# Output projection in twelve pieces in slots 9 to 14 of a layer's attention pipeline; second norm, routing and slot table one period later

## The chip, the cores and the metric

The kernel runs on one core of a Trainium2 chip, and its time is the device time of one execution in microseconds (us). The profile calls the engines PE (TensorE, matrix products; PEld is its weight loads), DVE (VectorE), ACT (ScalarE), POOL (GpSimd) and SP (SyncE, which only issues transfers here; SPq is its queue). Each engine runs its own instructions in program order, and engines wait for each other on semaphores.

## The reference

The reference makes 256 token rows per sequence with a state-space kernel, appends 128 text rows, and runs one transformer layer over 8 sequences of 384 rows of 512 values. The state-space part is a phase of its own and is not touched.

```python
h = jnp.concatenate([state_space(x), txt], axis=1)                  # (8, 384, 512)
h = h + attention(layernorm(h), Wq, Wk, Wv, Wo)                     # 16 heads of 32, 4 key/value heads
h = h + ffn(layernorm(h), gate_w, w_gate, w_up, w_down, ...)        # 64 experts, top 6, 64 slots each
...
scores = jnp.einsum('bhqd,bhkd->bhqk', q, k) * scaling
out = jnp.einsum('bhqk,bhkd->bhqd', softmax(scores), v)
attn = jnp.einsum('bsh,oh->bso', out, Wo)                           # the output projection
...
topk_w, topk_i = jax.lax.top_k(softmax(x @ gate_w.T), 6)            # routing
pos = position of each (token, expert) pair among the pairs of its expert
valid = pos < 64                                                    # a pair has a slot, or is dropped
```

## The kernel before

The program has three phases: the state-space phase, the attention phase, and the experts' phase, which starts when the attention phase has ended. The change is in `attention_phase` alone.

**A software pipeline over sequences.** The attention phase takes one sequence of 384 rows (NT = 3 tiles of 128) at a time. The outer loop runs over b, and each pass, called a period here, works on up to four sequences at once: b itself (`main`: scores, exponentials, values), the next, a = b + 1 (`nxt`: its projections, its rotary turn, its row maxima), the one before, c = b - 1 (`prev`: output projection, residual, second norm), and d = b - 2 (`prev2`: router logits, top 6, positions, slot table). Passes in which a role has no sequence leave it out.

**Slots.** Each period has NH = 16 slots, n = 0 to 15, one for each head. Each engine has the same loop over b and n, written by hand, with `if` lines that say what it does in which slot. That alone sets the order on an engine. On TensorE a slot starts with `scores(b, n)` (L634), three matmuls over 97 rows into PSUM banks 0 to 2. ScalarE then takes the exponentials (L808), and `values` (L650) multiplies them with the values and with ones four heads at a time, in three of every four slots: slots 3, 7, 11 and 15 have none.

**Row maxima.** The softmax needs each row's maximum ahead of the scores. In slots 8 to 15 TensorE computes the scores of the next sequence a first time, in bf16 (`raw`, L664), 48 units in all, six a slot, into two PSUM banks in turn. VectorE reduces each (`row_maximum`, L951). Unit u can't start before the maximum of unit u - 2 has been taken. The maxima are transposed in slot 12 and in slot 0 of the next period (`turn_maxes`, L670) and join the score matmuls as their 97th row.

**Around the change.** `project_out(c, s)` multiplies tile s of the attention output, split into a high and a low part (`out_hi` on ScalarE, `out_lo` on GpSimd, both after `divide` on VectorE), with the weights: 12 matmuls of 512 columns through `product`. It is done in slots 6, 7 and 8 (`OUT_SLOT`), and VectorE adds the residual one slot later. `statistics2` (L975) in slot 9, a power on GpSimd (L1108) and three activations (L870) give the normed rows x2; `turn_x2` (L724) transposes them in slots 12 to 15, each step waiting for ScalarE's copy (L876) of the one before, as all share PSUM bank 7. In the next period follow the router `logits` (L731) in slot 0, `routing` on VectorE in slots 1, 2, 4, 5 and 9, whose middle part (L996 to L1002) builds a mask of the chosen experts, and `places` (L739) on TensorE in slot 4. GpSimd works the positions out (L1081 to L1087) in slot 6. VectorE turns them into slot numbers in slot 9, and GpSimd scatters them into the slot table with 18 indirect DMAs (L1114), three in each of slots 10 to 15.

**Heads.** `rope` on VectorE and `rope_sum` on GpSimd (L1072) turn the queries and keys of the next sequence, one tile at a time. In slot 7 `turn_heads` (L706) transposes them in five steps; ScalarE copies each twice and VectorE takes the low part (`q_lo`, L940), and a step waits for the one two before it. The first raw scores wait for all of that.

## Time and profile before

| | us |
|---|---|
| Median of 3 runs | 1705.49 (1704.61 to 1706.07) |
| The profiled execution's own time | 1706.95 |
| Its span in the profile | 1705.3 |
| TensorE busy | 1368.9 |
| VectorE busy | 759.1 |
| ScalarE busy | 404.9 |
| GpSimd busy | 424.6 |

### The profile page before, as it was taken

The numbers are of one execution on the slowest core, as the hardware profiler recorded it, in microseconds if no ns is written. First come the engines' busy times: TensorE is split into PE (matmuls) and PEld (weight loads), VectorE is DVE, ScalarE is ACT, GpSimd is POOL, SyncE is SP. The second block draws the span as 40 slices with busy tenths as digits, with TensorE's granted clock in tenths as the row PEclk, the third lists the DMA queues.
The fourth block names the chain that finished last, engine by engine and source line by source line (L and its number), as shares of the span: only waits on it lengthen the run. The fifth ranks groups of instructions, "written<-read, shape, count | busy, mean of one in ns | idle before, by whom it ended". The sixth has DMA issues, their size and how long they took to land. (4 is left out here: it accounts for less than half of the span.)

```text
span 1705.3 us, 23870 instructions
## 1 busy us (share of the span) xinstructions
PE 1368.9 (80%) x9120; PEld 843.2 (49%) x9120; DVE 759.1 (45%) x1633; ACT 404.9 (24%) x676; POOL 424.6 (25%) x455
## 2 busy tenths in 40 slices
PE   3094788879788788887978840499999999999994
PEld 2094452434426254352533430366666666666673
DVE  7982545455555656456455331332232222232231
ACT  2021123333333233333333410211111111111110
POOL 3000110100242223324233446122222222222221
...
DMA packets 129837, 239.54 MB, mean 140 GB/s; under 512 B 58056, under 2 KB 64088, under 8 KB 129752
## 3 DMA queue, kind: packets, MB, share of 16 engines
...
## 5 line engine op out<-in xcount | busy, mean ns | idle before, releaser
L951 DVE TENSOR_REDUCE at_maxes<-at_ps 128x1 f32<-128x384 f32 x384 | 196.4, 553 | 131.3 <-PE at_ps L664 122.6
L808 ACT ACTIVATE bulk<-at_ps 128x1152 f32<-128x1152 f32 x128 | 144.9, 1132 | 367.4 <-PE at_ps L634 367.1
L1313 PE MATMUL mo_ps<-mo_x2s,mo_sgu 128*117 128x384 f32 (+1 forms) x1152 | 221.2, 344 | 0.0
L1313 PEld LDWEIGHTS mo_ps<-mo_x2s,mo_sgu 128*117 128x117 f32 (+1 forms) x1152 | 198.7, 181 | 13.4 <-issue 13.1
L1534 POOL DMA_INDIRECT out_rows<-mo_y,mo_scatter_ix x64 | 91.4, 1428 | 399.6 <-DMA out_rows<-mo_y,mo_scatter_ix 226.1
L664 PE MATMUL at_ps<-at_qb 32*128 32x384 bf16 x384 | 125.7, 442 | 78.6 <-DVE at_maxes L951 59.5
L1114 POOL DMA_INDIRECT slot_table<-at_toki,at_si x144 | 141.2, 981 | 51.0 <-issue 48.3
L664 PEld LDWEIGHTS at_ps<-at_qb 32*128 32x128 bf16 x384 | 28.6, 96 | 211.0 <-DVE at_maxes L951 173.5
L624 PE MATMUL at_ps<-WxT,at_xT 128*128 128x512 f32 (+1 forms) x576 | 114.0, 351 | 17.4 <-ACT at_v L853 15.6
L634 PE MATMUL at_ps<-at_QT 97*128 97x384 f32 x384 | 115.5, 416 | 6.9 <-ACT bulk L808 6.9
L1076 POOL TENSOR_TENSOR at_oTs<-at_oT,at_oTs 128x384 fp32r<-128x384 f32 x32 | 32.1, 1002 | 352.0 <-ACT at_oTs L820 352.0
L624 PEld LDWEIGHTS at_ps<-WxT,at_xT 128*128 128x128 f32 x576 | 90.0, 192 | 48.7 <-issue 34.5
L1327 PE MATMUL mo_ps<-mo_sd,mo_hs 117*128 117x512 f32 (+1 forms) x432 | 105.5, 397 | 3.6 <-DVE mo_so L1476 3.6
L650 PE MATMUL at_ps<-bulk,at_v 128*32 128x384 f32 x768 | 103.1, 629 | 3.4 <-DVE at_oT L964 2.7
L371 PE MATMUL ss_psK<-ss_Q,bulk 64*64 64x64 f32 x2048 | 62.7, 222 | 49.4 <-DVE bulk L320 48.4
L650 PE MATMUL at_ps<-bulk,at_ones 128*32 128x384 f32 x768 | 96.3, 598 | 0.0
L1327 PEld LDWEIGHTS mo_ps<-mo_sd,mo_hs 117*128 117x128 f32 (+1 forms) x432 | 79.4, 188 | 26.2 <-DVE mo_so L1476 5.6
L1498 DVE SCALAR_TENSOR_TENSOR mo_hm<-mo_sil,mo_wcol,mo_ps 128x352 f32<-128x352 f32 x32 | 18.6, 581 | 163.4 <-ACT mo_sil L1426 163.4
L634 PEld LDWEIGHTS at_ps<-at_QT 97*128 97x128 f32 x384 | 75.2, 224 | 30.3 <-issue 16.7
L624 PE MATMUL at_ps<-WoT,at_oTs 128*128 128x512 f32 x288 | 85.4, 453 | 5.4 <-DVEq L1015 3.4
L1355 PE MATMUL mo_ps<-mo_wgu,mo_xgT 128*64 128x352 f32 x512 | 82.0, 474 | 9.4 <-DMA mo_wd<-in_L_ffn_w_down 9.4
L371 PEld LDWEIGHTS ss_psK<-ss_Q,bulk 64*64 64x64 f32 x2048 | 62.2, 139 | 49.9 <-issue 49.9
...
## 6 DMA issues: line engine op xcount, KB each, us to landing
...
```

The source lines that it names most:

```text
L371: m = T.matmul(psK[half, n % 2, i * STEP:(i + 1) * STEP], Pm[half, k % 2, t, h, :], basis, start=(t == 0), stop=(t == 3))
L624: m = T.matmul(out, xs[:, xa, k, x_cols], ws[:, wa, k, w_cols], start=(n == 0), stop=(n == 3 * KC - 1))
L634: m = T.matmul(ps[:, kt, 0:SEQ], QT[:, NH + h // REP, kt * P:(kt + 1) * P], QT[:, h, :], start=True, stop=True)
L650: m = T.matmul(ps[HD * j:HD * (j + 1), 3 + sums, 0:SEQ], w, PT[:, (REP * G + j) % RING, kt, :], start=(kt == 0), stop=(kt == NT - 1))
L664: T.matmul(ps[:, 5 + u % 2, 0:SEQ], qb[rows, r, s * P:(s + 1) * P], qb[rows, REP, :], start=True, stop=True).then_inc(raw_scores, 1)
L808: A.activation(PT[:, N % RING, :, :], ps[:, 0:NT, 0:SEQ], ACT.Exp, scale=float(HD) ** -0.5)\
L951: V.tensor_reduce(maxes[:, s, h:h + 1], ps[:, 5 + u % 2, 0:SEQ], AX.X, ALU.max, negate=True)\
L1114: G.indirect_dma_start(slot_table, bass.IndirectOffsetOnAxis(ap=si[:, m:m + 1], axis=0), toki[:, m // TOPK:m // TOPK + 1], None, bounds_ch ...
L1313: m = M.matmul(ps[0:SW[c], 5 + g, 0:SEQ], sgu[:, wa, g, k, SO[c]:SO[c] + SW[c]], x2s[:, xa, k, :], start=(k3 == 0), stop=(k3 == 3 * KC - 1))
L1327: m = M.matmul(ps[:, 7, :], hs[0:SW[c], xa, c, s * P:(s + 1) * P], sd[0:SW[c], wa, c, :], start=(k3 == 0), stop=(k3 == 3 * SC - 1))
L1355: m = M.matmul(ps[CAP * e:CAP * (e + 1), 1 + g, 0:I], xgT[:, k, CAP * e:CAP * (e + 1)], wgu[j][:, e, g, k, :], start=(k == 0), stop=(k == ...
L1534: G.indirect_dma_start(acc, bass.IndirectOffsetOnAxis(ap=scatter_ix[:, qix, e:e + 1], axis=0), y[:, jy, e, :], None, compute_op=ALU.add).t ...
```

## The change

The output projection of a tile is cut into four pieces of three matmuls. The twelve pieces of the three tiles go into slots 9 to 14, two a slot: one behind the second pair of raw scores, one behind the third. The outputs of the first two groups of heads are kept in a ring of four and split in slot 15, since the projection now reads the split buffer until slot 14. Residuals move to slots 11, 13 and 15. The second norm moves from slot 9 to slots 0 and 1 of the next period, the transposes of x2 to slots 3 and 4, the logits to slot 5, the routing to slots 6, 7, 9 and 10, the places to slot 8 (TensorE) and slot 10 (GpSimd). The slot numbers and the scatters move one period further, into slots 1 to 6 of the period of e = b - 3, and the loop gets one pass more. SyncE stores the turned rows before the scores' rows and moves the store of h behind the maxima's row.

```diff
-        OUT_SLOT = {6: 0, 7: 1, 8: 2}
+        OUT_FROM = 9
+        OUT_SLOT = {OUT_FROM + 1: 0, OUT_FROM + 3: 1, OUT_FROM + 5: 2}
+        TURN_SLOT = {3: (0, 1), 4: (2, 3)}
+        DIVIDED = {0: (-2,), 4: (-1,), NH - 1: (0, 1)}
...
-        ITERATIONS = range(-1, B + 2)
+            return tuple(0 <= b - k < B for k in range(-1, 4))
+
+        ITERATIONS = range(-1, B + 3)
...
+                    sp.wait_ge(x2T_ready, KC * (d + 1))
+                    sp.dma_start(x2T_dram[d], x2T[:]).then_inc(x2T_stored, 16)
...
-            def project_out(c, s):
-                if s == 0:
+            def project_out(c, i):
+
+                s, piece = i // 4, i % 4
+                if i == 0:
                     pe.wait_ge(ohi_ready, NKV * (c + 1))
                     pe.wait_ge(olo_ready, NKV * (c + 1))
                     wait(pe, pos_read, c)
-                wait(pe, h2_ready, NT * c + s)
-                product(ps[:, 7, :], oTs, slice(s * P, (s + 1) * P), WoT, slice(0, D)).then_inc(proj_done, 1)
+                if piece == 0:
+                    wait(pe, h2_ready, NT * c + s)
+                m = product(ps[:, 7, :], oTs, slice(s * P, (s + 1) * P), WoT, slice(0, D),
+                            range(3 * KC // 4 * piece, 3 * KC // 4 * (piece + 1)))
+                if piece == 3:
+                    m.then_inc(proj_done, 1)
...
+                    pieces = range(2 * (n - OUT_FROM), 2 * (n - OUT_FROM + 1)) if prev and OUT_FROM <= n < OUT_FROM + 6 else ()
                     if main:
                         scores(b, n)
+                    if prev2 and n in TURN_SLOT:
+                        turn_x2(d, TURN_SLOT[n][0])
...
+                    if prev2 and n == 8:
+                        places(d)
+                    for i in pieces[0:1]:
+                        project_out(c, i)
...
-                    if prev2 and n == 0:
+                    if prev2 and n == 5:
...
-                    if prev2 and n == 4:
-                        places(d)
-                    if prev and n in OUT_SLOT:
-                        project_out(c, OUT_SLOT[n])
...
-                    if prev and n >= NH - KC:
-                        turn_x2(c, n - (NH - KC))
+                    if prev2 and n in TURN_SLOT:
+                        turn_x2(d, TURN_SLOT[n][1])
                     for u in units[4:]:
                         raw(a, u)
+                    for i in pieces[1:2]:
+                        project_out(c, i)
...
+            def x2_copied(d, k):
+                act.wait_ge(x2_turned, KC * d + k + 1)
+                wait(act, x2T_stored, 16 * d)
+                A.activation(x2T[:, k, :], ps[:, 7, 0:SEQ], ACT.Copy).then_inc(x2T_ready, 1)
+
             def out_hi(G):
                 act.wait_ge(o_ready, G + 1)
                 wait(act, proj_done, NT * (G // NKV))
-                A.activation(oTs[:, 0, G % NKV, :], oT[:, G % 2, :], ACT.Copy).then_inc(ohi_ready, 1)
+                A.activation(oTs[:, 0, G % NKV, :], oT[:, G % NKV, :], ACT.Copy).then_inc(ohi_ready, 1)
...
-                    if n in (0, 4, 9, 13):
-                        G = NKV * b + {0: -2, 4: -1, 9: 0, 13: 1}[n]
-                        if 0 <= G < NKV * B:
-                            out_hi(G)
+                    if prev2 and n in TURN_SLOT:
+                        x2_copied(d, TURN_SLOT[n][1])
+                    for k in DIVIDED.get(n, ()):
+                        if 0 <= NKV * b + k < NKV * B:
+                            out_hi(NKV * b + k)
...
-                if n == 1:
+                if n == 6:
...
-                if n == 2:
+                if n == 7:
...
-                if n == 4:
+                if n == 10:
...
-                if n == 5:
+                if n == 9:
...
+            def slots(e):
+                dve.wait_ge(slot_rows_ready, e + 1)
+                link(V.tensor_reduce(sf[:], hv[:], AX.X, ALU.add), route_step)
+                wait(dve, scattered, 16 * NT * TOPK * e)
...
+                    if prev and n - 1 in OUT_SLOT:
+                        residual(c, OUT_SLOT[n - 1])
                     if n % REP == REP - 1:
                         divide(NKV * b + n // REP - 1)
-                    if prev and n - 1 in OUT_SLOT:
-                        residual(c, OUT_SLOT[n - 1])
                     if nxt and n == 0:
                         for k in range(KC):
                             x_lo(a, k)
+                    if prev2 and n == 0:
+                        statistics2(d)
+                    if prev3 and n == 1:
+                        slots(e)
...
-                    if prev2 and n == 6:
+                    if prev2 and n == 10:
                         places(d)
-                    if prev and n == 9:
-                        pool.wait_ge(var2_ready, c + 1)
+                    if prev2 and n == 0:
...
-                    if prev2 and n >= 10:
-                        pool.wait_ge(slots_ready, d + 1)
-                        for m in range(3 * (n - 10), 3 * (n - 9)):
+                    if prev3 and 1 <= n <= 6:
+                        pool.wait_ge(slots_ready, e + 1)
+                        for m in range(3 * (n - 1), 3 * n):
```

The line numbers of the changed kernel differ: L625 is its `product`, L730 `turn_x2`, L737 `logits`, L745 `places`, L954 `q_lo`, L965 `row_maximum`, L985 the residual, L1011 to L1017 the masks, L1090 `rope_sum`, L1094 `out_lo`, L1131 the scatters.

How TensorE's order changes is seen in slot 9 of a full period, with the last rows of slot 8 ahead of it. L634 are scores, L664 raw scores, L650 values, L624 and L625 the output projection. Before:

```order
L624 MATMUL at_ps<-WoT,at_oTs 128x512 x12
L664 MATMUL at_ps<-at_qb 128x384 x2
L634 MATMUL at_ps<-at_QT 128x384 x3
L664 MATMUL at_ps<-at_qb 128x384 x2
L650 MATMUL at_ps<-bulk,at_v 32x384 x4
L664 MATMUL at_ps<-at_qb 128x384 x2
L650 MATMUL at_ps<-bulk,at_ones 32x384 x4
L664 MATMUL at_ps<-at_qb 128x384 x2
L634 MATMUL at_ps<-at_QT 128x384 x3
```

After, the same slot, from its scores (slot 8 has no projection):

```order
L634 MATMUL at_ps<-at_QT 128x384 x3
L664 MATMUL at_ps<-at_qb 128x384 x2
L650 MATMUL at_ps<-bulk,at_v 32x384 x4
L664 MATMUL at_ps<-at_qb 128x384 x2
L625 MATMUL at_ps<-WoT,at_oTs 128x512 x3
L650 MATMUL at_ps<-bulk,at_ones 32x384 x4
L664 MATMUL at_ps<-at_qb 128x384 x2
L625 MATMUL at_ps<-WoT,at_oTs 128x512 x3
L634 MATMUL at_ps<-at_QT 128x384 x3
```

The block of twelve projection matmuls of slot 8 is gone, and slot 9 has two pieces of three, the first behind the second pair of raw scores and the second behind the third pair.

GpSimd's order from the scatters of one full period to its positions. Before (L1114 scatters, L1076 `out_lo`, L1072 rotary sums, L1081 to L1087 positions):

```order
L1076 TENSOR_TENSOR at_oTs<-at_oT,at_oTs 128x384
L1114 DMA slot_table<-at_toki,at_si 4096x1 x9
L1076 TENSOR_TENSOR at_oTs<-at_oT,at_oTs 128x384
L1072 TENSOR_TENSOR at_r<-at_r 128x640
L1076 TENSOR_TENSOR at_oTs<-at_oT,at_oTs 128x384
L1072 TENSOR_TENSOR at_r<-at_r 128x640 x2
L1081 TENSOR_TENSOR at_pos<-at_pos,at_slot 128x192
L1083 TENSOR_TENSOR at_pos<-at_pos,at_over 128x192
L1087 TENSOR_TENSOR at_hv<-at_hot,at_pos 128x384 x3
```

After (L1131 scatters, L1090 rotary sums, L1094 `out_lo`, L1125 and L1127 the second norm):

```order
L1094 TENSOR_TENSOR at_oTs<-at_oT,at_oTs 128x384 x3
L1125 TENSOR_TENSOR at_rstd<-at_ve,at_mhalf 128x3
L1127 TENSOR_TENSOR at_shift<-at_shift,at_rstd 128x3
L1131 DMA slot_table<-at_toki,at_si 4096x1 x6
L1090 TENSOR_TENSOR at_r<-at_r 128x640
L1131 DMA slot_table<-at_toki,at_si 4096x1 x3
L1094 TENSOR_TENSOR at_oTs<-at_oT,at_oTs 128x384
L1090 TENSOR_TENSOR at_r<-at_r 128x640
L1131 DMA slot_table<-at_toki,at_si 4096x1 x6
L1090 TENSOR_TENSOR at_r<-at_r 128x640
L1131 DMA slot_table<-at_toki,at_si 4096x1 x3
L1083 TENSOR_TENSOR at_rstd<-at_ve,at_mhalf 128x3
```

Fifteen of the eighteen scatters now stand ahead of the third rotary sum, where none stood, and the power of the second norm stands ahead of the first of them.

VectorE's order around slots 7 and 8 (L940 and L954 the low parts of the heads, L970 a residual, L951 and L965 row maxima). Before:

```order
L964 TENSOR_TENSOR at_oT<-at_ps,at_rsums 128x384
L970 TENSOR_TENSOR at_hr<-at_hr,at_ps 128x512
L940 TENSOR_TENSOR at_qlo<-at_ps,at_qhi 128x384 x5
L970 TENSOR_TENSOR at_hr<-at_hr,at_ps 128x512
L951 TENSOR_REDUCE at_maxes<-at_ps 128x1 x6
L970 TENSOR_TENSOR at_hr<-at_hr,at_ps 128x512
```

After (L1011 to L1017 the masks, L1027 to L1029 the positions):

```order
L979 TENSOR_TENSOR at_oT<-at_ps,at_sT 128x384
L954 TENSOR_TENSOR at_qlo<-at_ps,at_qhi 128x384 x5
L1011 TENSOR_TENSOR at_hot<-at_iota,at_mf 128x384 x3
L1016 TENSOR_REDUCE at_pos<-at_hot 128x192
L1017 CAST at_mask<-at_pos 128x192
L965 TENSOR_REDUCE at_maxes<-at_ps 128x1 x6
L1027 TENSOR_TENSOR at_pos<-at_ps,at_base 128x192
L1028 TENSOR_SCALAR at_over<-at_pos 128x192
L1029 TENSOR_TENSOR at_base<-at_base,at_ps 128x64
L965 TENSOR_REDUCE at_maxes<-at_ps 128x1 x6
```

The masks now stand between the low parts of the heads and the first row maxima, and the residuals left that place.

## Rows read from the trace of the kernel before

**Rows 1.** The page, part 1: busy time, share of the span, instructions, by engine.

```profile
PE 1368.9 (80%) x9120; PEld 843.2 (49%) x9120; DVE 759.1 (45%) x1633; ACT 404.9 (24%) x676; POOL 424.6 (25%) x455
```

**Rows 2.** Windows, b = 4: length, busy PE, PEld, DVE, ACT, POOL, clock, DMA.

```profile
608.00:643.78 35.78, 32.23 (x220) 21.71 (x219) 16.76 (x48) 12.33 (x24) 5.08 (x4) 0.90 0.53 133
643.78:659.66 15.88, 12.39 (x66) 9.03 (x65) 8.32 (x22) 7.16 (x14) 6.44 (x8) 0.89 0.00 1
659.66:665.46 5.80, 5.80 (x34) 2.93 (x34) 2.45 (x5) 0.33 (x1) 0.00 (x0) 1.00 0.71 148
665.46:674.46 9.00, 5.42 (x27) 1.41 (x25) 8.47 (x20) 1.54 (x2) 1.84 (x2) 0.74 0.57 158
674.46:679.89 5.43, 5.43 (x26) 1.53 (x25) 2.60 (x5) 3.24 (x4) 3.92 (x5) 0.50 0.01 0
679.89:685.54 5.65, 3.29 (x11) 1.10 (x9) 5.18 (x11) 1.13 (x1) 4.14 (x5) 0.80 0.02 0
685.54:694.36 8.82, 7.60 (x32) 2.35 (x31) 2.71 (x6) 1.94 (x3) 0.97 (x1) 0.50 0.02 4
694.36:710.39 16.03, 13.69 (x71) 4.97 (x69) 10.93 (x22) 6.56 (x10) 9.77 (x10) 0.71 0.01 0
```

**Rows 3.** Timeline of TensorE, period of b = 4: start, us, instructions, idle before.

```profile
645.83 3.08 PE L624 MATMUL at_ps<-WoT,at_oTs 128*128 128x512 f32 x12
...
666.90 0.85 PE L650 MATMUL at_ps<-bulk,at_v 128*32 128x384 f32 x8
...
674.46 1.33 PE L634 MATMUL at_ps<-at_QT 97*128 97x384 f32 x3
...
676.15 1.51 PE L650 MATMUL at_ps<-bulk,at_ones 128*32 128x384 f32 x8
...
683.50 0.96 PE L664 MATMUL at_ps<-at_qb 32*128 32x384 bf16 x2 [2.09 <-DVE at_maxes L951]
```

**Rows 4.** Timeline of TensorE: slots 6 and 8 of b = 0; starts of three periods.

```profile
252.16 0.69 PE L634 MATMUL at_ps<-at_QT 97*128 97x384 f32 x3
...
262.28 0.63 PE L664 MATMUL at_ps<-at_qb 32*128 32x384 bf16 x2 [0.64 <-ACT at_qhi L864]
...
307.24 1.33 PE L634 MATMUL at_ps<-at_QT 97*128 97x384 f32 x3
...
403.37 1.33 PE L634 MATMUL at_ps<-at_QT 97*128 97x384 f32 x3
...
915.17 1.33 PE L634 MATMUL at_ps<-at_QT 97*128 97x384 f32 x3
```

**Rows 5.** Timeline of GpSimd, period of b = 4.

```profile
644.68 1.56 POOL L1072 TENSOR_TENSOR at_r<-at_r 128x640 f32<-128x640 f32 x1 [4.65 <-DVE at_r L934]
...
676.60 0.98 POOL L1114 DMA_INDIRECT slot_table<-at_toki,at_si  x1 [0.30 <-issue]
```

**Rows 6.** Timeline of VectorE, b = 4: split of x, masks (first, last), statistics.

```profile
615.36 1.13 DVE L911 TENSOR_TENSOR at_xT<-at_ps,at_xT 128x384 fp32r<-128x384 f32 x2 [1.71 <-ACT at_xT L837]
...
625.36 1.49 DVE L996 TENSOR_TENSOR at_hot<-at_iota,at_mf 128x384 bf16<-128x384 f32 x3
...
629.19 0.26 DVE L1002 CAST at_mask<-at_pos 128x192 bf16<-128x192 f32 x1
...
671.03 1.87 DVE L975 BATCH_NORM_STATS2 at_bn<-at_hr 128x6 f32<-128x512 f32 x3
```

**Rows 7.** Timeline after the last scores: last scores, logits, projection, a copy, last scatter.

```profile
971.46 0.77 PE L634 MATMUL at_ps<-at_QT 97*128 97x384 f32 x3
...
974.94 2.89 PE L731 MATMUL at_ps<-gwT,at_x2T 128*128 128x64 f32 x24
...
988.19 5.46 PE L624 MATMUL at_ps<-WoT,at_oTs 128*128 128x512 f32 x12 [3.42 <-DVEq L1015]
...
1011.02 0.49 ACT L876 ACTIVATE at_x2T<-at_ps 128x384 f32<-128x384 f32 x1 [0.99 <-PE at_ps L724]
...
1061.81 0.97 POOL L1114 DMA_INDIRECT slot_table<-at_toki,at_si  x1 [0.30 <-issue]
```

103 lines of the change are left out of this document (44 added, 59 removed).

## The prediction

> **What bounds the kernel now.** The page's first part comes first [rows 1]. TensorE is busy for 1368.9 us of 1705.3 and VectorE for 759.1, so TensorE's stream is the one to follow. The attention phase runs a pipeline of eight sequences with one period for each. The next thing to find is what one period costs and where TensorE stands idle or slow in it.
>
> Periods are read from the first score matmul of each sequence. They start at 307.24 (b = 1), 403.37 (b = 2) and 915.17 (b = 7) [rows 4]. So b = 1 lasts 96.1 us, and b = 2 to 6 last 511.8 / 5 = 102.4 us each. That makes five equal periods, one that is different, one that the change leaves alone (b = 0), and a tail.
>
> The period of b = 4 is then cut at its slots, the stretches between one head's scores and the next [rows 2]. Slots 0 to 5 (35.8 us) are TensorE's own: 32.2 us busy at a mean clock of 0.90. Slots 6 and 7 (15.9 us) wait on the chain that turns the heads. Slots 8 to 15 (50.7 us) are mixed. In slot 9 VectorE is busy 8.5 of 9.0 us and TensorE 5.4; in slot 11 VectorE has 5.2 of 5.7. In slots 10 and 12 TensorE is busy but runs at 0.50 of its clock. A group of value matmuls takes 0.85 us at full clock and 1.51 at half, and half-clock scores take 1.33 against 0.69 [rows 3, 4]. So the second half loses time in two ways. TensorE waits for row maxima (2.09 us in slot 11 alone [rows 3]), and it works at 1.2 GHz after such waits.
>
> **Slots 0 to 5.** The logits (2.89 us [rows 7], 2.7 without the overlap) leave slot 0 and enter slot 5. The four groups of x2 transposes enter slots 3 and 4 at some 0.4 us each; half of them fall into the wait for the values' copy. The place matmuls (0.3) leave. The sum is +0.2, so 36.0 us. VectorE gets the second norm's statistics (1.9 us for their first step [rows 6], some 2.7 in all) and the slot columns (an estimate of 2.2) there, about 5 us, while it is busy for only 16.8 of 35.8 us [rows 2], so I cost them at nothing for VectorE itself.
>
> **GpSimd.** This queue isn't free. Its 18 scatters cost 0.98 + 0.30 = 1.28 us each [rows 5] and stood in slots 10 to 15, where nothing waited for them. Now fifteen are issued in program order before the third rotary sum, for which the head transposes of slot 7 wait. GpSimd can start them when VectorE has made the slots. VectorE's split of x ends at 616.5, 8.5 us into the period [rows 6]; with statistics and slots behind it that is 13.5 us. To this come 15 x 1.28 = 19.2 us, one output residue of 1.0, three sums of 1.56 [rows 5], and a wait of about 4.5 us, since the residue in slot 4 now stands behind the last x2 copy on ScalarE, which comes with the end of slot 4, and the scatters issued by then fill less than the time up to it. The total is 42.9 us. Slot 6 begins at 36.0, so the sum ends 6.9 us after it. Before, it ended at 646.24, which is 2.5 us after slot 6 began at 643.78 [rows 2, 5]. GpSimd is 4.4 us late there. The lower bound is no lateness (the wait vanishes and DMA issues run closer), the upper one 7 us.
>
> **Slots 6 and 7.** They took 15.9 us with two output projections of about 3 us in them, one of which stretched the chain of head transposes. In b = 0, where no projection stands there, slots 6 and 7 take 262.28 - 252.16 = 10.1 us [rows 4]. With GpSimd's lateness, part of which is covered by VectorE (which now has 1.7 us of routing before its work on the heads and is late by some 2.4 us itself), I take 14.0 us: 1.9 saved. The bounds are 10.1 + 2.4 = 12.5 and 17.
>
> **Slots 8 to 15.** A projection of 12 matmuls takes 3.08 us at full clock [rows 3] and 5.46 at mostly half [rows 7]. A piece of three is then 0.75 or 1.35 us. Of each slot, before [rows 2] and now:
> - Slot 8, 5.8 us: it loses a projection, but VectorE must now build the slot masks (625.36 to 629.45, 4.1 us [rows 6]) before its first row maximum. TensorE has two score matmuls' work and then waits about 3.4 us. Then six maxima of 0.55. I take 7.9 us.
> - Slot 9, 9.0 us: VectorE loses residual, statistics and slots, about 5 us. TensorE's own work with two pieces is 4.8 us at full clock, 8.0 at half. I take 5.9.
> - Slot 10, 5.4 us at half clock: with pieces 5.0 at full clock.
> - Slot 11, 5.65 us: the wait for VectorE's division stays (residual in front of it fits into the time it had free). The first piece stands behind the wait and not in it. I take 7.3, since the clock should fall there again; 5.9 if not.
> - Slot 12, 8.8 us: minus one group of transposes (0.8), plus two pieces. All slow it is 10.5, all fast 7.4. I take 8.4.
> - Slots 13 to 15, 16.0 us with three groups of transposes: slots 13 and 14 take 9.5 at full clock with four pieces, and 16 at half. Slot 15 keeps its division and six maxima, 5.6. I take 15.1.
>
> The sum is 49.6 us against 50.7 (7.9 + 5.9 + 5.0 + 7.3 + 8.4 + 15.1). The period comes to 36.0 + 14.0 + 49.6 = 99.6 us, 2.8 less, and five of them give 14. In b = 1 no routing, second norm or scatter is moved in yet, so slots 6 and 7 fall from 15.9 to 10.1, and slots 8 to 15 stay within 0.2 us: -5.6 us, 90.5 us.
>
> **The tail.** The program goes one iteration longer. Before, x2 of sequence 6 was transposed between the scores of b = 7, and its logits began at 974.94 [rows 7]. Now its last residual comes with slot 15 of b = 7, whose scores ran at 971.46 [rows 7]; the projection pieces go where the x2 chain held b = 7 up, so I put it at 970.5 on the old clock. Then division, statistics, GpSimd's power and three activations (8.5 us) follow, and four steps of transposing and copying, 0.99 + 0.49 = 1.5 us each, by the copy and its wait [rows 7]: the logits begin at 985. From logits to the last sequence's projection it was 988.19 - 974.94 = 13.3 us [rows 7]; one division no longer stands in that stretch, so 11 to 13. The projection then begins at 996 to 998, 8 us later. What follows it (statistics, 18 scatters, places, slots, 18 scatters up to 1061.81 [rows 7]) has the same order as before. A third block of 18 scatters (23 us, for sequence 5) now stands in the tail, but I expect it from 978 to 1002, while the chain above goes on without GpSimd. So +8 us, between +4 and +12.
>
> **Sum.** -14 - 5.6 + 8 = -11.6 us. The profiled execution took 1706.95 us around its span of 1705.3, 1.46 us over the median of 1705.49. 1706.95 - 11.6 = 1695.3, and against the median 1693.9. I round to 1694 us.
>
> **Rivals.**
> - The clock stays high (0.22). If the pieces let TensorE leave half clock early in slot 9 and keep it through slot 11's wait, slots 9 to 15 cost 3.5 us less. With no more than VectorE's lateness in slots 6 and 7 (1.5 less) that gives 94.6 us a period: five times 7.8, 8 in b = 1 (its 5.6 and some clock), less 8 in the tail, is 39 us gained, 1667. For it: the pieces fill slots where 5.4 us of 5.4 were busy with matmuls of a quarter of the array's columns or rows. The Trainium skill ("TensorE: Matmul & The Clock Gate", What's actually happening) says that the default state is throttled and activity releases the throttle. Slot 10, busy throughout at 0.50, shows that busy time alone did not do it here [rows 2].
> - The clock stays low (0.16), the slower side. Slot 8 now has a wait of over 3 us, before it TensorE has only transposes, and slots 11 and 15 keep theirs. If half clock holds in slots 9, 12 and 13 as in [rows 2] it did in 10 and 12, they cost 8.0 + 10.5 + 6.3, some 6 us more than in my sum. The period is 105.6 us: five times +3.2, no gain in b = 1 and +8 in the tail come to +24, 1729. It decides once it costs more than 2.5 us a period over my sum.
> - The third block of scatters is exposed (0.09). If its slots are ready 11 us later than I think, half of it adds to the end: +12 us, no change, 1706.
> - GpSimd isn't late and the clock is as forecast: 98.1 us a period, five times 1.5 less, 1686; this lies inside my case.
>
> **Chances and range.** My case, from 1682 to 1704, holds 0.50, and 0.03 is left for what I have not thought of. Over 0.2% (3.4 us), about what a measurement of this kernel can tell from none, counts as a difference. Faster: 0.22 and most of 0.50 make 0.69. Same: 0.12. Slower: 0.19. The range reaches almost to the high-clock case and about half of the way to the low-clock one: 1671 to 1714.
>
> **What would show it.** In the changed profile I expect periods of 99 to 100 us between first scores, and about 90 for b = 1. Slots 6 and 7 should be 14 us, with the head transposes released by GpSimd's rotary sum; if VectorE releases them, my GpSimd count is wrong. The wait for maxima in slot 8 should be over 3 us, released by VectorE behind the masks. Granted clock in slots 9 to 14 should be above 0.75. The last projection should start near 977 (996 to 998 less the 20 us gained by then, so 977), and the last scatter 8 us later relative to the first score of b = 7. I am wrong if the clock in slots 9 to 14 is the same as before or lower, or if the period stays near 102 us.

## The result and the profile after

The changed kernel takes 1717.49 us (median of 4 runs, 1714.98 to 1720.21) against 1705.05 us (4 runs, 1702.19 to 1706.07) of the kernel before: a ratio of 1.0073, 95% interval 1.0057 to 1.0089. It is 12.4 us slower, where 11.6 us less were forecast. The span of the profiled execution is 1716.7 us against 1705.3.

Part 1 of the page after, to be held against [rows 1]:

```profile
PE 1377.3 (80%) x9120; PEld 852.8 (50%) x9120; DVE 764.3 (45%) x1633; ACT 405.0 (24%) x676; POOL 423.5 (25%) x455
```

TensorE does the same 9120 matmuls in 8.4 us more of busy time. The timeline of TensorE after, with the first score matmuls of b = 1, 2, 4 and 7 and the last scores, shows where in the phase the time goes:

```profile
305.77 1.01 PE L634 MATMUL at_ps<-at_QT 97*128 97x384 f32 x2
396.88 1.01 PE L634 MATMUL at_ps<-at_QT 97*128 97x384 f32 x2
604.35 1.33 PE L634 MATMUL at_ps<-at_QT 97*128 97x384 f32 x3
915.00 1.33 PE L634 MATMUL at_ps<-at_QT 97*128 97x384 f32 x3
974.01 0.69 PE L634 MATMUL at_ps<-at_QT 97*128 97x384 f32 x3
```

| stretch | before [rows 4, 7] | after | forecast |
|---|---|---|---|
| b = 1 | 96.1 | 91.1 | 90.5 |
| b = 2 to 6, mean | 102.4 | 103.6 | 99.6 |
| b = 7 start to last scores | 56.3 | 59.0 | 55.3 |
| last scores to last scatter | 90.35 | 99.1 | 99.3 |

The last two forecasts follow from the 970.5 us and the +8 us of the prediction. b = 1 won its 5 us. The next five periods lost 6.3 us together, b = 7 another 2.7 and the tail 8.75. The last row of GpSimd's timeline stands for the end of the phase:

```profile
1073.11 0.97 POOL L1131 DMA_INDIRECT slot_table<-at_toki,at_si  x1 [0.30 <-issue]
```

That is 11.3 us behind the 1061.81 of [rows 7].

The windows of b = 4 after, with the columns of [rows 2], cut at slots 0 and 6, close to the first raw scores, and at slots 9 to 13; the last line is slots 9 to 14 in one. The first raw scores start at 655.26, 0.26 us behind the third cut:

```profile
604.35:641.15 36.80, 34.11 (x223) 23.05 (x222) 13.87 (x37) 14.12 (x22) 16.89 (x17) 0.88 0.39 96
641.15:655.00 13.85, 7.75 (x42) 4.76 (x40) 10.69 (x31) 7.08 (x15) 9.42 (x10) 0.72 0.02 1
655.00:662.86 7.86, 5.39 (x31) 1.40 (x31) 5.87 (x10) 1.84 (x7) 0.00 (x0) 0.50 0.01 3
662.86:669.74 6.88, 6.88 (x33) 2.98 (x32) 4.42 (x11) 1.13 (x1) 3.85 (x5) 0.65 0.00 0
669.74:674.82 5.08, 5.01 (x33) 2.21 (x31) 3.71 (x11) 1.13 (x1) 0.00 (x0) 1.00 0.65 214
674.82:682.61 7.79, 5.30 (x17) 2.76 (x16) 5.79 (x12) 1.13 (x1) 0.00 (x0) 0.70 0.80 163
682.61:691.98 9.37, 8.02 (x36) 3.10 (x34) 3.02 (x6) 1.61 (x2) 0.00 (x0) 0.70 0.02 4
691.98:707.57 15.59, 12.81 (x72) 5.27 (x70) 11.59 (x24) 6.32 (x8) 1.95 (x2) 0.93 0.24 73
662.86:702.12 39.26, 35.22 (x175) 15.47 (x174) 23.43 (x51) 8.66 (x9) 3.85 (x5) 0.81 0.25 61
```

The clock in slots 9 to 14 is 0.81, as hoped; before it was 0.65:

```profile
665.46:704.62 39.16, 31.88 (x148) 9.90 (x146) 25.08 (x53) 12.02 (x16) 16.71 (x18) 0.65 0.14 37
```

But the same stretch is no shorter, since the pieces are in it, and ahead of it the clock fell: slots 6 and 7 from 0.89 to 0.72, slot 8 from 1.00 to 0.50 [rows 2]. Slot 0 alone went from 0.67 to 0.50.

In slots 6 to 8 the whole projections of before stood between TensorE's waits for the heads and the maxima. The pass of b = 1 shows what their removal does nearly by itself, since neither kernel has routing, places or scatters in it. Its slots 8 and 9, before:

```profile
352.76:362.06 9.30, 7.78 (x41) 3.62 (x39) 3.66 (x7) 2.62 (x5) 0.00 (x0) 0.82 0.50 103
362.06:368.42 6.36, 4.09 (x28) 1.34 (x26) 6.19 (x16) 1.54 (x2) 1.71 (x2) 1.00 0.74 209
```

After:

```profile
345.75:351.97 6.22, 5.58 (x28) 1.62 (x26) 2.92 (x6) 2.00 (x3) 0.00 (x0) 0.50 0.50 100
351.97:358.96 6.99, 6.99 (x33) 2.98 (x32) 3.77 (x8) 1.13 (x1) 0.00 (x0) 0.63 0.61 125
```

Slot 8 is 3.1 us shorter without its projection, but runs at 0.50 instead of 0.82, and slot 9 enters at the low clock and has a mean of 0.63 instead of 1.00.

Rows of TensorE and GpSimd in slots 7, 8 and 11 of b = 4:

```profile
647.75 1.51 PE L706 MATMUL at_ps<-at_ident,at_r 128*128 128x128 f32 x6 [3.77 <-issue]
659.51 0.96 PE L664 MATMUL at_ps<-at_qb 32*128 32x384 bf16 x2 [2.21 <-DVE at_maxes L965]
678.26 0.96 PE L664 MATMUL at_ps<-at_qb 32*128 32x384 bf16 x2 [2.48 <-DVE at_maxes L965]
646.12 1.54 POOL L1090 TENSOR_TENSOR at_r<-at_r 128x640 f32<-128x640 f32 x1
```

The head transposes start 0.09 us after the third rotary sum ends at 647.66, and idle 3.77 us ahead of them. The waits for maxima in slots 8 and 11, 2.21 and 2.48 us, have nothing in them.

### The profile page after: what moved, and what is told of

It reads as the page before. It is cut to its first block and busy times, and to the rows that moved or that the text cites. A ratio compares the mean times of both kernels' runs of the same rounds, so it can differ in the third digit from the quotient of the medians.

```text
span 1716.7 us, 23894 instructions
## 1 busy us (share of the span) xinstructions
PE 1377.3 (80%) x9120; PEld 852.8 (50%) x9120; DVE 764.3 (45%) x1633; ACT 405.0 (24%) x676; POOL 423.5 (25%) x455
## 5 line engine op out<-in xcount | busy, mean ns | idle before, releaser
L965 DVE TENSOR_REDUCE at_maxes<-at_ps 128x1 f32<-128x384 f32 x384 | 196.5, 553 | 131.9 <-PE at_ps L664 124.8
L1551 POOL DMA_INDIRECT out_rows<-mo_y,mo_scatter_ix x64 | 91.3, 1427 | 406.0 <-DMA out_rows<-mo_y,mo_scatter_ix 185.8
L664 PE MATMUL at_ps<-at_qb 32*128 32x384 bf16 x384 | 113.6, 419 | 69.4 <-DVE at_maxes L965 55.1
L1131 POOL DMA_INDIRECT slot_table<-at_toki,at_si x144 | 141.7, 984 | 58.4 <-issue 47.1
L1094 POOL TENSOR_TENSOR at_oTs<-at_oT,at_oTs 128x384 fp32r<-128x384 f32 x32 | 31.7, 1004 | 402.9 <-ACT at_oTs L836 402.8
L664 PEld LDWEIGHTS at_ps<-at_qb 32*128 32x128 bf16 x384 | 26.8, 95 | 204.6 <-DVE at_maxes L965 152.0
L625 PE MATMUL at_ps<-WxT,at_xT 128*128 128x512 f32 (+1 forms) x576 | 114.6, 352 | 12.7 <-ACT at_v L866 11.0
L650 PE MATMUL at_ps<-bulk,at_v 128*32 128x384 f32 x768 | 113.0, 683 | 3.2 <-DVE at_oT L979 3.2
L634 PE MATMUL at_ps<-at_QT 97*128 97x384 f32 x384 | 113.5, 411 | 2.2 <-ACT bulk L819 2.2
L625 PE MATMUL at_ps<-WoT,at_oTs 128*128 128x512 f32 x288 | 109.4, 502 | 3.1 <-DVE at_hr L985 2.0
L625 PEld LDWEIGHTS at_ps<-WxT,at_xT 128*128 128x128 f32 x576 | 90.5, 193 | 40.7 <-issue 26.3
L634 PEld LDWEIGHTS at_ps<-at_QT 97*128 97x128 f32 x384 | 80.1, 230 | 29.7 <-issue 16.4
L650 PE MATMUL at_ps<-bulk,at_ones 128*32 128x384 f32 x768 | 84.2, 529 | 0.0
```

The source lines that it names most:

```text
L625: m = T.matmul(out, xs[:, xa, k, x_cols], ws[:, wa, k, w_cols], start=(n == 0), stop=(n == 3 * KC - 1))
L634: m = T.matmul(ps[:, kt, 0:SEQ], QT[:, NH + h // REP, kt * P:(kt + 1) * P], QT[:, h, :], start=True, stop=True)
L650: m = T.matmul(ps[HD * j:HD * (j + 1), 3 + sums, 0:SEQ], w, PT[:, (REP * G + j) % RING, kt, :], start=(kt == 0), stop=(kt == NT - 1))
L664: T.matmul(ps[:, 5 + u % 2, 0:SEQ], qb[rows, r, s * P:(s + 1) * P], qb[rows, REP, :], start=True, stop=True).then_inc(raw_scores, 1)
L965: V.tensor_reduce(maxes[:, s, h:h + 1], ps[:, 5 + u % 2, 0:SEQ], AX.X, ALU.max, negate=True)\
L1131: G.indirect_dma_start(slot_table, bass.IndirectOffsetOnAxis(ap=si[:, m:m + 1], axis=0), toki[:, m // TOPK:m // TOPK + 1], None, bounds_ch ...
```

## Experiments

Batches fell on two levels: the kernel before took 1705 us in some and 1732 to 1735 us in others, so a ratio is read within its level. Unless said otherwise an edit is made to the changed kernel, and lengths of slots are from one head's first scores to the next, in b = 4.

**The yardsticks, at 1733 us.** The changed kernel again:

> The changed kernel unaltered, as the yardstick for the three that follow on the same chip. All theories: 1.007 of the kernel before. If this chip shows the second half of slot 3 and slot 11 long by 2 to 3 us each, as the runs with the masks, the matmuls for the clock and the early pieces did, then those stalls belong to the chip and not to the edits.

Measured: 1719.98 us, 0.9921 (0.9901 to 0.9942) of the kernel before, which took 1732.37. The same pair of programs has the other sign here. The expected 1.007 was wrong. Of the rest half came: slot 3 was 6.3 to 6.6 us in b = 3 to 5 instead of 4.4 and slot 4 6.5 to 6.8 instead of 5.9, while slot 11 stayed at 7.1 to 8.1, about as at 1705 us. The kernel before, to see where its 27 us are:

> The kernel before unaltered, for its profile on the kind of chip on which it takes 1730 to 1735 us instead of 1705. Theory 'scatters beside a burst of DMA stall the core there': its scatters stand in slots 10 to 15, as in scatter_late, so slots 10 to 12 of periods b=3 to 6 are 4 to 7 us longer than on the first chip, all other slots the same to 0.2 us. Rival 'everything is a little slower there': each slot is longer by 1 to 2 per cent.

Measured: 1733.53 us, 1.0001 (0.9986 to 1.0015) of the same kernel beside it. Both theories fell. Slots 0 to 13 of b = 4 are as at 1705 us, to 0.1 us; windows of slots 13, 14 and 15:

```profile
698.33:704.60 6.27, 6.27 (x31) 2.04 (x29) 3.07 (x6) 2.04 (x4) 2.76 (x3) 0.50 0.00 0
704.60:710.86 6.26, 6.26 (x30) 2.03 (x28) 3.06 (x6) 1.99 (x3) 4.74 (x6) 0.50 0.02 0
710.86:718.12 7.26, 4.46 (x15) 1.83 (x13) 4.83 (x10) 2.65 (x4) 2.24 (x3) 0.50 0.01 0
```

At 1705 us the clock was back at 1.00 in slot 14 (4.02 us for the same work); here it stays at 0.50 through slot 15. b = 3 does the same. In b = 2, 5 and 6 slot 14 takes 4.02 us as before and slot 15 8.0 to 9.0 instead of 5.8, so the low clock is not the whole of it. Of the 25 us between the two profiled spans some 15 are in these two slots, 4.3 in b = 7 and 7.7 behind the last scores, while b = 1 is 3.3 shorter.

**GpSimd's queue.** Scatters in slots 10 to 15, as before the change:

```diff
-                    if prev3 and 1 <= n <= 6:
+                    first = 10 if nxt else 1
+                    if prev3 and first <= n < first + 6:
...
-                        for m in range(3 * (n - 1), 3 * n):
+                        for m in range(3 * (n - first), 3 * (n - first + 1)):
```

> While a next sequence exists, the 18 scatters go back to slots 10 to 15 of GpSimd's loop, behind the rotary sums (the passes of the tail keep them in slots 1 to 6). Theory 1, GpSimd's queue: the third rotary sum is no longer late, the 3.8 us wait ahead of the head transposes goes, slots 6 and 7 fall from 12.2 to some 10.2 us as in the period of b = 2, which has no scatters, in four periods: about -8 us, 1709. Theory 2, the granted clock: the time that is freed comes back as half clock in other slots, as in b = 2 (102.8 us against 103.8 on average of the four later ones): -4 us or less, 1713 to 1717.

Measured, at 1733 us: 1.0013 (0.9992 to 1.0033), slower than the changed kernel's 0.9921. Slots 6 and 7 fell from 12.2 to 10.2, as theory 1 has it, but slot 11 took 13.7 instead of 7.8:

```profile
676.40:690.10 13.70, 6.29 (x16) 2.93 (x15) 5.79 (x11) 1.13 (x1) 9.36 (x10) 0.65 0.43 94
```

The scatters ran beside the burst of transfers that stacks the queries, and TensorE stood for 5.8 us, ScalarE for 8.0 and VectorE for 2.5. So the scatters were put between the third rotary sum and the places instead, six in each of slots 7 to 9:

```diff
-                    if prev3 and 1 <= n <= 6:
+                    per, first = (6, 7) if nxt else (3, 1)
+                    if prev3 and first <= n < first + 18 // per:
...
-                        for m in range(3 * (n - 1), 3 * n):
+                        for m in range(per * (n - first), per * (n - first + 1)):
```

> The changed kernel with only that move of the scatters. Theory 'GpSimd's queue': slots 6 and 7 10.2 instead of 12.2, nothing else moved, 2 us of each of four or five periods and on this kind of chip slot 3's 2 us of three periods as well: 1.007 becomes 1.000 there, and here, where the changed kernel is 0.992 of the kernel before, 0.983 to 0.987. Rival 'the clock gives it back': slot 9 takes 0.5 to 1.5 us more in each period, and 0.988 to 0.992.

Measured, at 1705 us: 1.0016 (1.0005 to 1.0027), against 1.0073. Slots 6 and 7 are 10.2, and b = 3 to 6 take 102.4 on average instead of 104.0: 1.6 of the 2.0 us arrive. That is a mean only: the four periods gain 2.8, 0.7, -0.5 and 3.5 us, since the changed kernel's own vary from 101.8 to 105.6 with the clock of slots 9 and 12. The rest of the gain lies in b = 7 (57.3 instead of 59.0) and outside the periods. That GpSimd's late sum costs 2.0 us in slots 6 and 7 is shown. The expected 1.000 was nearly reached, and the kernel before is still not beaten.

**Whole projections.** All four pieces of a tile at the end of slots 10, 12 and 14:

```diff
-                    pieces = range(2 * (n - OUT_FROM), 2 * (n - OUT_FROM + 1)) if prev and OUT_FROM <= n < OUT_FROM + 6 else ()
+                    pieces = range(4 * OUT_SLOT[n], 4 * OUT_SLOT[n] + 4) if prev and n in OUT_SLOT else ()
...
-                    for i in pieces[0:1]:
-                        project_out(c, i)
...
-                    for i in pieces[1:2]:
+                    for i in pieces:
                         project_out(c, i)
```

> The change without its division into pieces: each product of the projection stands whole (twelve matmuls) at the end of slots 10, 12 and 14. Theory 'pieces behind waits': a three-matmul piece at either end of a slot fills nothing, since its slot's last row maximum releases the next raw product at once, so the whole products cost the same TensorE time: within 3 us of the changed kernel. Rival 'the division feeds the granted clock or fills the waits': slots 10, 12 and 14 take 3 us more each and slots 9, 11 and 13 less than that back, the period 1 to 2 us longer and the kernel 6 to 12 us slower than the changed one.

Measured, at 1733 us: 0.9955 (0.9938 to 0.9971), 4.9 us over the changed kernel there, with b = 3 to 6 equal to 0.2 us (105.9 and 105.8). That lies between the theory (within 3 us) and the rival (6 to 12), and the intervals overlap. Cutting into pieces is worth little where the pieces stand.

**A piece in the wait.** The first piece of a slot goes ahead of its second pair of raw scores:

```diff
+                    for i in pieces[0:1]:
+                        project_out(c, i)
                     for u in units[2:4]:
                         raw(a, u)
...
-                    for i in pieces[0:1]:
-                        project_out(c, i)
```

> The first projection piece of each slot is issued ahead of the second pair of raw scores and no longer behind it. Theory 1, placement: in slot 11 it fills 0.8 to 1.3 us of the 2.5 us wait for row maxima, in slot 12 the 0.65 us wait, and TensorE's gap is shorter, so that the clock falls less: slots 11 and 12 lose some 2 us together, six periods, about -12 us, 1705. Rival: where TensorE and not VectorE is the later one (slots 9, 10, 13, 14), the piece delays raw scores and so the maxima: nothing gained or up to 1 us a period lost, 1717 to 1723.

Measured, at 1733 us: 0.9849 (0.983 to 0.9868), 0.7% or some 12 us better than the changed kernel, as theory 1 forecast. Windows of slots 11 and 12, which took 7.8 and 9.5 at clocks of 0.71 and 0.70:

```profile
671.05:677.05 6.00, 4.03 (x16) 1.98 (x15) 5.44 (x11) 1.13 (x1) 0.00 (x0) 0.99 0.86 175
677.05:684.63 7.58, 7.01 (x36) 2.84 (x34) 2.85 (x6) 1.61 (x2) 0.00 (x0) 0.78 0.10 22
```

**Filling with work that nobody reads.** First only ahead of the turned heads, then in all waits of slots 7 and 8:

```diff
+            def warm(d, count):
+                pe.wait_ge(lg_copied, d + 1)
+                for _ in range(count):
+                    T.matmul(ps[:, 7, :], xT[:, 0, 0, 0:P], WxT[:, 0, 0, 0:512], start=True, stop=True)
...
+                    if nxt and prev2 and n == 7:
+                        warm(d, 14)
```

warm_through adds 4 such matmuls in each of two more places of slot 7, and 4 and 8 in slot 8.

> 14 matmuls of 512 columns on the full array that nobody reads stand in slot 7 behind the scores, where TensorE waits 3.8 us for GpSimd's rotary sum; they go to PSUM bank 7, which is free there. They add 3.4 us of TensorE work and cover a wait, nothing else changes. Theory 2, the granted clock: TensorE enters the head transposes and slot 8 at full clock, the windows of slots 8 and 9 show above 0.8 in place of 0.50 and 0.65, and slots 7 to 9 fall by about 3 us in each of five periods: 1702. Rival, the clock is not what costs: no change or a few us more, 1717 to 1722.

> The changed kernel with idle-filling matmuls, whose results nobody reads, in all of TensorE's waits of slots 7 and 8: 14 of 512 columns ahead of the turned heads, 4 after each of two pairs of them, 4 ahead of the first raw product, 8 ahead of the second pair of raw products. Theory 'the granted clock takes the freed time back after each wait': with the waits filled slots 8 and 9 run near 1.00 instead of 0.50 and 0.65, slot 9 falls from 7.0 to 5.1 and slot 8 by 1 us or more, the period by 3 us, the kernel by 15 us or more, although work was added. Rival 'the waits set the length and the clock is only a symptom': the filling adds its own time, slot 9 stays near 7, and the period is the same or 1 to 2 us longer.

Measured, at 1733 us: warm14 0.9917 (0.9897 to 0.9937), no change; its slot 7 ran at 0.90 and slot 8 at 0.50 all the same. warm_through 0.9855 (0.9824 to 0.9886), 11.2 us less than the changed kernel for more work. Its slots 7, 8 and 9:

```profile
641.21:650.78 9.57, 8.07 (x44) 5.93 (x41) 8.01 (x25) 4.57 (x11) 7.90 (x9) 1.00 0.02 1
650.78:659.18 8.40, 7.03 (x49) 3.70 (x48) 6.80 (x11) 2.87 (x9) 0.00 (x0) 1.00 0.00 1
659.18:667.01 7.83, 7.83 (x33) 2.96 (x32) 4.51 (x11) 1.13 (x1) 3.86 (x5) 0.56 0.01 2
```

Slots 7 and 8 rose to 1.00 and slot 8 took 8.4 instead of 9.55. In this period slot 9 then fell to 0.56; in b = 2 it was 6.05 us at 1.00, never the 5.1 expected. The kernel gained 11 us where 15 or more were expected, and not where the theory had them: over b = 2 to 6, slot 8 gave 5.8 us and slot 9 nothing, while slot 12, which has no filler near it, gave 8.8 (7.2, 6.9 and 6.9 us in b = 4 to 6 instead of 9.5, 9.2 and 10.8).

**Pieces in both waits.** One piece each between the first two pairs of raw scores in slots 10 to 15; the third residual at the start of the next period.

```diff
+        OUT_SLOT = {OUT_FROM + 2: 0, OUT_FROM + 4: 1}
+        PIECES = {9: ((), (0,)), 10: ((1,), (2,)), 11: ((3,), ()), 12: ((4,), (5,)),
+                  13: ((6,), (7,)), 14: ((8,), (9,)), 15: ((10,), (11,))}
+        DIVIDED = {0: (-4, -3, -2), 4: (-1,)}
...
+                    for i in mid:
+                        project_out(c, i)
                     for u in units[2:4]:
                         raw(a, u)
...
                     if prev2 and n == 0:
+                        residual(d, 2)
                         statistics2(d)
```

> The twelve pieces laid otherwise: one each between the two first pairs of raw products in slots 10 to 15, so also in slots 11 and 15, in which VectorE divides and TensorE waited 2.5 us; the last residual of a sequence moves to the start of the next period, and the high parts of its first two head groups too. Theory 'pieces must stand in the waits': slots 11 and 12 come to 6.0 and 7.5 as in piece_first, and after slot 15 the clock stays up, so slot 0 falls from 8.4 to 7 to 7.5: 1 to 3 us a period better than piece_first, which was 0.985 of the kernel before. Rival 'the last residual delays the split of x or the second norm': slots 0 and 3 grow by what slot 15 gives.

Measured, at 1733 us: 0.9751 (0.9717 to 0.9786), 1691.4 us. Slots 0, 3 and 11:

```profile
579.18:584.97 5.79, 4.37 (x35) 2.18 (x33) 1.64 (x4) 3.50 (x7) 0.00 (x0) 1.00 0.01 3
596.40:607.49 11.09, 4.21 (x23) 3.97 (x21) 2.16 (x8) 1.68 (x3) 6.30 (x6) 0.71 0.69 153
653.71:657.82 4.11, 3.10 (x14) 1.31 (x12) 4.01 (x9) 1.13 (x1) 0.00 (x0) 1.00 0.86 178
```

Against the changed kernel at this level slot 0 is 5.8 instead of 8.5 and slot 11 4.1 instead of 7.8, while slot 3 is 11.1 instead of 6.4. Two periods have no stall in slot 3: b = 2 takes 91.6 us instead of 102.0, and b = 6, where slot 0 is at 0.56 again, 99.4 instead of 105.0. By the ratios it is 1.0%, some 17 us, better than piece_first, 2.4 us a period, where the theory had 1 to 3. But this comes unevenly, since with the stall b = 4 and 5 are 1.5 and 3.0 us longer than there.

**Together, at 1705 us.** Three versions, each with one edit on top of two_waits: the load of the residual rows moved off slot 3 (two_hr_late), the filling added (two_warm), the scatters in slots 7 to 9 (two_mid):

> two_waits with the load of the residual rows (768 KB) moved from slots 2 and 3 to slot 5, behind the store of the turned rows. In two_waits slot 3 was 4.4 us in the periods without scatters or without a load of x, and 8.9 to 11.1 in b=3 to 5, which have both. Theory 'the load of the residual rows beside the scatters stalls the core': slot 3 falls to 4.4 in b=3 to 5 and no other slot grows by more than 1 us, 4 to 6 us a period, 14 to 18 us in all. Rival 'scatters stall beside any load': the stall moves to slot 5 or 6, or stays in slot 3, and the time is within 3 us of two_waits.

> two_waits and the filling matmuls of warm_through together. Theory 'the clock takes the freed time back after each unfilled wait': the two gains are in different slots and add, slots 8 and 9 come to 8.4 and 5.1 to 7.5 and slots 12 and 0 stay at 6.2 and 5.8: 10 to 15 us below two_waits. Rival 'the clock falls somewhere else for each place that is filled': within 4 us of two_waits, with another slot at 0.50 that was at 1.00.

> two_waits with the eighteen scatters of a sequence in slots 7 to 9, six a slot, behind the rotary sum of the third block instead of ahead of it. Theory 'scatters beside loads stall slot 3, and scatters ahead of the rotary sum cost slots 6 and 7 two us': slot 3 4.4 and slots 6 and 7 10.2 together instead of 12.2, in all periods, 6 to 9 us a period where the stall was, 25 to 30 us in all. Rival 'the scatters take VectorE's or the places' time wherever they stand': slots 8 to 10 grow by what is gained, above all because the places of the slots on GpSimd stand behind the scatters.

Measured: two_hr_late 0.9866 (0.982 to 0.9911), two_warm 0.9732 (0.9679 to 0.9785), two_mid 0.9714 (0.9689 to 0.9739), with medians of 1677.5, 1658.5 and 1654.4 us. Slot 3 was 4.4 in all three, also in two_warm, where neither scatters nor load had moved: the stall isn't there at this level, so none of them tests it. Means of b = 3 to 6: 98.4, 92.7 and 92.6. In two_warm slots 8 and 9 came to 8.4 and 5.1 as expected, but slot 12 took 8.7 to 9.1 us in b = 2, 4 and 5 and slot 0 7.7 to 7.8 in b = 3, 5 and 6, so its rival came in part too. From the first version to the third the late rotary sum goes, 2.0 us in slots 6 and 7 (the load also stands in slots 2 and 3 again, with slot 3 at 4.4 in both), and the period loses 5.9: slots 0 and 12 took 7.8 and 8.6 in two_hr_late, and in two_mid, in windows of slots 0, 7, 8, 9, 11 and 12:

```profile
573.02:578.82 5.80, 4.38 (x36) 2.19 (x34) 1.65 (x4) 3.51 (x7) 0.00 (x0) 1.00 0.01 3
608.86:616.97 8.11, 3.55 (x23) 2.89 (x19) 6.19 (x25) 4.56 (x11) 5.51 (x8) 0.71 0.01 0
616.97:626.51 9.54, 6.69 (x36) 2.20 (x34) 6.43 (x11) 2.99 (x9) 7.41 (x8) 0.50 0.03 4
626.51:633.43 6.92, 6.92 (x31) 2.73 (x29) 5.16 (x14) 1.13 (x1) 5.33 (x6) 0.50 0.02 0
639.71:643.82 4.11, 3.10 (x13) 1.31 (x11) 4.01 (x9) 1.13 (x1) 0.00 (x0) 1.00 0.84 174
643.82:650.07 6.25, 5.68 (x36) 2.58 (x35) 4.12 (x9) 1.61 (x2) 0.00 (x0) 1.00 0.16 34
```

In b = 3 to 5 one stretch at the low clock is left; in b = 6 slot 12 is at 0.56 again. All three edits together (pieces in the waits, scatters in slots 7 to 9, filling):

> two_waits, the scatters of two_mid in slots 7 to 9, and the filling matmuls of warm_through (6 instead of 14 ahead of the turned heads, since there is less to wait for). Theory 'each unfilled wait costs its own clock': slot 7 8.1, slot 8 8.4, slot 9 5.1, slot 10 5.1 to 5.8, so 3 to 4 us a period below two_mid, 16 to 22 us in all, 0.960 to 0.963 of the kernel before. Rival 'one episode at the low clock a period stays': slot 12 goes to 9 as in two_warm, and the time is that of two_mid to 6 us.

Measured: 0.9633 (0.9616 to 0.965), 1642.8 us, the best of all. Slots 8, 9, 11 and 12, this time of b = 3:

```profile
527.12:535.51 8.39, 6.99 (x49) 3.68 (x46) 6.80 (x11) 2.87 (x9) 6.31 (x7) 1.00 0.02 0
535.51:540.65 5.14, 4.60 (x30) 1.92 (x29) 4.36 (x11) 1.13 (x1) 3.87 (x4) 1.00 0.02 0
545.73:549.84 4.11, 3.10 (x13) 1.31 (x11) 4.01 (x9) 1.13 (x1) 3.60 (x5) 1.00 0.70 169
549.84:558.41 8.57, 8.00 (x35) 2.87 (x35) 4.01 (x9) 1.61 (x2) 0.00 (x0) 0.60 0.36 73
```

The rival was right in part: slots 8 and 9 came down as expected and slot 12 went to 8.6 to 9.8 at 0.50 to 0.60, behind a slot 11 that is the same as in two_mid, where slot 12 was at 1.00. b = 3 to 6 take 91.3 instead of 92.6, and the two profiled spans are 1648.0 and 1649.0: the slowest of the four executions of three and the fastest of those of two_mid. So the 11.6 us between the medians, where 16 to 22 were expected, can't be found in these two traces.

**Masks.** Chosen experts by comparison with the sixth largest logit, one-hot rows built in slot 9:

```diff
...
+                        ins = V.tensor_scalar(mask[:, s, :], lg[:, s, :], mx[:, s, TOPK - 1:TOPK], None, ALU.is_ge)
+                    ins.then_inc(mask_ready, 1)
...
                 if n == 9:
+                    for s in range(NT):
+                        ins = V.tensor_tensor(
+                            hot[:, s * TOPK:(s + 1) * TOPK, :],
...
```

> The mask of the chosen experts is made in slot 7 by comparing the logits with the sixth largest (three operations on 64 columns, some 0.6 us) in place of the three comparisons and the reduction of 4.1 us; the comparisons that GpSimd's positions need move to slot 9, the reduction is gone. Theory 3, VectorE ahead of the first row maxima: the wait of slot 8 (2.2 us after one of 0.6) goes, slot 8 falls by 3 us in five periods, and the tail loses two times 3.5 us, since both of its chains run through the mask: about -22 us, 1695. If the clock takes it back elsewhere, only the tail's 7 us and some of the rest remain, 1705 to 1710. If the masks are covered anyway: 1710 from the tail alone.

> three with the masks from a comparison with the sixth largest logit, and the one-hot rows built in slot 9. Alone, on the changed kernel, this took 2.7 us from slot 8 and gave 2.9 us to slot 9, which ran at 0.50. Theory 'the clock took it back there': with the clock up in slots 8 and 9 slot 8 falls by 1.5 to 2.5 us and slot 9 is bound by the row maxima and one-hot rows on VectorE, 5.1 to 6.5: 1 to 2 us a period below three. Rival 'VectorE's work of slots 8 and 9 is the same sum and sets both': within 0.5 us a period of three.

Measured: alone, at 1733 us, 0.9899 (0.9878 to 0.9919), which overlaps the changed kernel's interval; slot 8 6.8 instead of 9.55, slot 9 9.9 instead of 7.0. From the last scores to the last scatter it took 103.9 us, where the changed kernel took 100.7 and 7 less were expected. On top of three 0.964 (0.9597 to 0.9683), no change: slots 8 and 9 are 6.8 and 7.2 instead of 8.4 and 5.15. TensorE with its filler is busy for 6.6 of the 6.8 us, and VectorE for 6.4 of the 7.2, so the filler bounds the one slot and VectorE, which now builds the one-hot rows there, the other.

**The tail.** Projection of sequence 7 into banks 0 to 2 behind logits (6), its residuals ahead of the places, the third scatter block behind the last low part; then the same with the piece in the wait, then with the scatters one slot sooner:

```diff
+                bank = s if c == B - 1 else 7
...
-                m = product(ps[:, 7, :], oTs, ...
+                m = product(ps[:, bank, :], oTs, ...
...
-                    if prev3 and 1 <= n <= 6:
+                    first = 5 if prev and not main else 1
+                    if prev3 and first <= n < first + 6:
```

> The changed kernel with another order behind the last scores only: projection (7) into banks 0 to 2, right behind logits (6), so that it no longer waits for the masks and places of sequence 6; its residuals ahead of the places on VectorE; the third block of scatters behind the low part of head group 31. Theory 'the added 11 us at the end are the projection's wait for the places of sequence 6': it starts at logits (6)'s end, near 992 instead of 1001 on the clock of the profile, and the end comes 7 to 9 us sooner, 1709 where the changed kernel has 1717. Rival 'the scatters of sequence 6 set the end': the block of sequence 6 starts no sooner, and the time moves by less than 2 us.

> The piece at the start of a slot ahead of its second pair of raw products, and the order of tail together. If the two costs are separate, their gains add: piece first gives 1 to 2 us of each of seven periods, about 8 to 12 us, and the end 7 to 9 us, so 15 to 21 us below the changed kernel and 3 to 9 us below the kernel before. If the clock takes back what the piece gives, only the end's share shows, 7 to 9 us.

> first_tail with the third block of scatters begun one slot sooner, so that the power for the last second norm does not stand behind three of them. Theory 'GpSimd's queue took back what the earlier projection gave': the last block of scatters starts 4 us sooner after the last scores than in first_tail, 96 to 97 us to the last scatter instead of 101, and the kernel takes 4 us less. Rival 'the last residual and the places of sequence 6, which came 6 us late there beside a burst of DMA, set it': no change over 1 us.

Measured, at 1733 us: 0.9941 (0.9923 to 0.9959), 0.9832 (0.98 to 0.9864) and 0.9847 (0.9815 to 0.988): no gain over after_again and piece_first. The projection started at 998.2 instead of 1008.8, as meant, but its third residual came late and the last norm's power stood in GpSimd's queue. VectorE and GpSimd of tail:

```profile
1008.14 0.69 DVE L990 TENSOR_TENSOR at_hr<-at_hr,at_ps 128x512 f32<-128x512 f32 x1 [3.15 <-remote]
1015.95 0.69 DVE L990 TENSOR_TENSOR at_hr<-at_hr,at_ps 128x512 f32<-128x512 f32 x1 [7.12 <-remote]
1025.01 0.92 POOL L1133 TENSOR_TENSOR at_rstd<-at_ve,at_mhalf 128x3 f32<-128x3 f32 x1
```

The last scatter came at 1081.05, and at 1080.82 in after_again: 101.5 and 100.7 us behind the last scores. What the third residual waited for between 1008.8 and 1015.9 the trace doesn't name.

## Why the prediction was wrong

- **Bounds.** The reading of TensorE's waits and low clock as the two losses held: every version that gained 1% or more over the changed kernel filled waits.
- **Slots 0 to 5**, 36.0 forecast, 36.8 measured (36.6 on average of b = 2 to 6). Slot 0 ran at 0.50 behind the unfilled wait of slot 15.
- **GpSimd and slots 6 and 7.** The sum was put 6.9 us behind the start of slot 6 and ended 647.66 - 641.15 = 6.5 behind it; 14.0 us to the first raw scores, 655.26 - 641.15 = 14.1 measured. scatter_mid shows the cause by taking it away.
- **Slots 8 to 15.** Slots 8, 10 and 11 came at 7.6, 5.1 and 7.8 (7.9, 5.0, 7.3 forecast). This is the step that failed, in its terms for slots 9 and 12: 5.9 and 8.4 forecast, 7.8 and 9.6 measured on average of b = 2 to 6. With 0.6 in slots 13 to 15 they make 3.8 of the 4.0 us by which a period was too long; what slots 0 to 5 lost, slots 6 to 8 gave back. I had slot 9 recover at once, though my own sum left slot 8 with a wait and no projection. It began at half clock. The work in these two terms was right: at a mean clock of 1.00 slot 9 takes 6.05 us (warm_through, b = 2), and slot 12 of b = 5, at 0.97, takes 7.1, near the 7.4 that I had for all fast. Slot 12 stood behind the empty wait of slot 11, but the wait alone doesn't settle its clock, as slot 12 of b = 3 and of b = 5 shows, behind waits of 2.48 and 2.84 us:

```profile
577.59:588.43 10.84, 9.62 (x36) 3.67 (x34) 3.07 (x6) 1.61 (x2) 0.00 (x0) 0.50 0.01 2
786.67:793.81 7.14, 5.79 (x35) 2.61 (x34) 2.70 (x6) 1.61 (x2) 0.00 (x0) 0.97 0.01 2
```

- **b = 1**: 90.5 forecast, 91.1 measured.
- **Tail**: +8 forecast, from the first score of b = 7 to the last scatter; 158.1 us against 146.6, so +11.5 measured, inside the 4 to 12 given. What follows the last scores came as put, 99.1 against 99.3. The rest is the pass of b = 7, whose scores now share TensorE with twelve pieces: put at 55.3 us, as if the pieces only filled what the x2 chain had held up, it took 59.0. The last projection, forecast near 977, started at 1000.94: 19 of these 24 us were there when b = 7 began (915.00, forecast 895.6), and 4 came behind that.
- **Rivals.** The low-clock rival came nearest. By its own point of decision, over 2.5 us a period above my sum, it holds, with 4.0 of its 6 us: slots 9 and 12 came near its 8.0 and 10.5, slot 13 (5.1 to 5.4) didn't run at half clock, and the kernel was at 1717 instead of 1729. The others didn't come: the clock was down in slots 7 to 9, GpSimd was late, and the third block of scatters, from 982 on, left the stretch behind the last scores at 99.1 us, as put.
- **Signs.** The clock did not stay low in slots 9 to 14 (0.81 against 0.65 in b = 4); what I named as the sign of success came true while the period didn't shrink, because low clock turned up in slots 7, 8 and 0. The mean over the period was 0.80 before and after in b = 4, and 0.78 after in b = 3 and 6. The wait for maxima in slot 8 was 2.2 us, where over 3 were named. The period was 103.6 us on average, and staying near 102 was named as a sign of being wrong.

Shown by experiments: that the late rotary sum costs 2.0 us in slots 6 and 7 of b = 3 to 6, of which 1.6 on average reach the period; that filling the waits of slots 11 and 15 keeps the clock up behind them in b = 2 (two_waits: 10.4 us) and in part in the later periods; and that in slots 7 and 8 filler without use buys back 11 us. That the whole projections of before had that filling role is seen in b = 1, where little else left slots 7 and 8, but no run put them back.
